# Gated cross-attention and a routed mixture of experts on one core: the two stages in one block, and the late logits read from where TensorE writes them

## The reference, cut to what matters

```python
x = x + jnp.tanh(g_xattn[0]) * xattn(ctx_1024, layernorm(x), ...)      # 8 x 112 x 256
t = layernorm(x)
logits = t @ Wg                                                        # 8 experts
P = softmax(logits); keep the two largest, P_norm = P_topk / (sum + 1e-9)
h = gelu(t @ W1[e] + b1[e]);  y_e = h @ W2[e] + b2[e]
x = x + jnp.tanh(g_ffn[0]) * sum_e P_norm[e] * y_e
```

## Time and profile before

| what | value |
|---|---|
| median of three runs | 502.27 us (501.06 to 504.05) |
| profiled execution, its own time | 500.76 us |
| its span (first to last instruction) | 499.0 us |
| mean granted TensorE clock | 0.931 of full speed |
| PE, DVE, ACT, POOL busy | 435.5, 286.8, 266.9, 198.3 us |

### The profile page before, as it was taken

One profiled execution on the slowest core, in us unless ns is written; L12 is line 12 of the kernel. 1 busy time (PEld: TensorE's weight loads), 2 busy tenths in 40 slices (PEclk: granted clock), 3 DMA queues, 4 the chain that ended last, 5 costly groups with the idle time before them and its releaser, 6 DMA issues. The chain is left out here.

```text
span 499.0 us, 9197 instructions
## 1 busy us (share of the span) xinstructions
PE 435.5 (87%) x3173; PEld 368.0 (74%) x3173; DVE 286.8 (57%) x707; ACT 266.9 (53%) x568; POOL 198.3 (40%) x219
## 2 busy tenths in 40 slices
PE   1899789999999999999995714899999999999990
PEld 1787557676767676767774513499999999999990
DVE  4654725363535444363447216298888888888840
ACT  3431147757575847566673110276776766676630
POOL 3440046555555565656402464002233333323222
PEclk9999979999999999999997555599999999999996
DMA  7300000001000199701700125586777878782313
GB/s 235 85 14 18 1 31 2 31 3 32 1 28 3 36 288 236 173 1 59 279 1 2 46 66 194 163 279 178 232 228 211 238 224 227 217 214 42 54 22 95
DMA packets 41864, 56.04 MB, mean 112 GB/s; under 512 B 1746, under 2 KB 37154, under 8 KB 41809
## 3 DMA queue, kind: packets, MB, share of 16 engines
q1 hardware_dynamic: 36848, 49.80, 32.6%
q0 software_dynamic: 4960, 5.72, 7.4%
q10 hardware_dynamic: 16, 0.00, 0.0%
HBM read 40.37 MB, written 16.07 MB: 113 GB/s over the span
## 5 line engine op out<-in xcount | busy, mean ns | idle before, releaser
L1379 POOL DMA_INDIRECT acc_scratch<-yv,xt x28 | 50.7, 1810 | 128.3 <-DVE yv L1532 124.0
L1401 ACT ACTIVATE hf<-ph,b1t 128x256 f32<-128x256 f32 x112 | 47.1, 472 | 47.9 <-PE ph L1607 47.2
L867 DVE TENSOR_REDUCE negmax<-sc 112x1 f32<-112x487 f32 x64 | 39.6, 660 | 49.5 <-PE sc L1115 49.5
L669 ACT COPY probt<-pt 125x448 f32<-125x448 f32 x64 | 34.3, 538 | 46.5 <-PE pt L1123 46.4
L661 ACT ACTIVATE prob<-sc,negmax 112x487 f32<-112x487 f32 x64 | 42.2, 664 | 24.9 <-DVE negmax L867 24.8
L1140 PEld LDWEIGHTS po<-probt,vals 125*64 125x64 f32 (+1 forms) x512 | 26.1, 142 | 23.0 <-issue 15.6
L1514 DVE TENSOR_TENSOR hl<-hf,hh 128x512 fp32r<-128x512 f32 x56 | 38.8, 692 | 1.9
L1123 PE MATMUL pt<-ident,prob 112*125 112x112 f32 x256 | 38.9, 276 | 0.0
L1123 PEld LDWEIGHTS pt<-ident,prob 112*125 112x125 f32 x256 | 36.0, 193 | 2.8
L1512 DVE CAST hh<-hf 128x512 fp32r<-128x512 f32 x56 | 24.2, 432 | 23.4 <-ACT hf L1401 23.0
L374 POOL TENSOR_TENSOR krot<-krow,rope_t 125x512 f32<-125x512 f32 x21 | 26.7, 1273 | 24.4 <-ACT krow L617 24.4
(11 more groups left out here) (303 smaller groups left out, 1295.2 us busy)
## 6 DMA issues: line engine op xcount, KB each, us to landing
w_first<-in_L_ffn_W SPq DMA_DIRECT2D x10, 1024.0 KB, 8.0
w_next<-in_L_ffn_W SPq DMA_DIRECT2D x10, 1024.0 KB
rows_scratch<-blank SPq DMA_DIRECT2D x2, 4257.0 KB, 32.2
w_third<-in_L_ffn_W SPq DMA_DIRECT2D x8, 1024.0 KB, 7.9
xt<-rows_scratch SPq DMA_DIRECT2D x14, 258.0 KB, 2.8
ctx_t<-in_ctx SPq DMA_DIRECT2D x8, 375.0 KB
w_first<-in_L_xattn_Wkv SPq DMA_DIRECT2D x1, 1024.0 KB, 9.2
x_all<-in_x SPq DMA_DIRECT2D x2, 448.0 KB, 4.1
```

The source lines that it names most:

```text
L669: act.copy(probt[:, h // 2 % 2, :, h % 2, :], pt[h % 2][0:JR, 0:NT * M].rearrange("q (a r) -> q a r", a=NT)) \
L867: dve.tensor_reduce(negmax[:, h % 2:h % 2 + 1], sc[h % 2][0:M, 0:JA], AX, ALU.max, negate=True).then_inc(max_done.sem, 1)
L1379: pool.indirect_dma_start(out=acc_dram, out_offset=bass.IndirectOffsetOnAxis(ap=xt[i % 3][:, n, D + 1:D + 2].bitcast(I32), axis=0), in_=yv ...
L1401: last = act.activation(hf[:, n % 3, u], ph[n % 3][:, u * T:(u + 1) * T], ACT.Gelu, bias=b1t[:, col])
```

## The change

Both functions now return their five instruction streams instead of opening a block; `build_program` opens one block, in which each engine runs its stream of attention and then its stream of experts. All semaphores are allocated in the outer scope. The memory that experts lays over attention's is guarded by two waits, whose values `attention` returns in `over_at`: SP waits for the last projection through Wo before it loads `b1rows`, and POOL waits for the last logits before it clears `b2x`. DVE no longer copies the late logits to `logit`; it runs `pick_first` on them in `pv`, at the end of attention's stream.

```diff
-        logit = keep("logit", [M, 2, E])
...
+        of_attention, over_at = attention(nc, sem, x, ctx, g_xattn, ...)
+        of_experts = experts(nc, sem, over_at, w1, b1, w2, b2, ...)
+        block = whole.enter_context(nc.Block())
+
+        @block.sync
+        def _(sp):
+            of_attention[0](sp)
+            of_experts[0](sp)
...
-        block = st.enter_context(nc.Block())
...
                 dve.wait_ge(logit_done, B)
-                dve.tensor_copy(logit[:], pv[0:M, (B - 2) * E:B * E].rearrange("q (b e) -> q b e", e=E))
+                router.pick_first(dve, pv[0:M, (B - 2) * E:B * E].rearrange("q (b e) -> q b e", e=E), LATE, 1)
...
+        last = B // 2 - 1, 1
+        over_at = dict(projected=(wo_done.sem, wo_done.at(*last, 1)), logits=(logit_done, B))
+        return (sync, gpsimd, scalar, vector, tensor), over_at
...
-        block = st.enter_context(nc.Block())
-        @block.sync
-        def _(sp):
+        def sync(sp):
+            sp.wait_ge(*over_at["projected"])
             sp.dma_start(b1rows[:], b1.rearrange("e (f p) -> (e f) p", p=P)).then_inc(small_loaded, 16)
...
             pool.memset(upto[:], 1.0).then_inc(ptables_set, 1)
+            pool.wait_ge(*over_at["logits"])
             pool.memset(b2x[:], 0.0).then_inc(b2x_set, 1)
...
-            router.pick_first(dve, logit[:], LATE, 1)
             router.pick_second(dve, LATE, 1)
```

More of the change, by code:

```diff
@@ L192, in build_program, with _, attention @@
         weights |= {n: [sem(f"{n}{r}") for r in range(RING)] for n in ("w1_loaded", "w2_loaded")}
-        attention(nc, x, ctx, g_xattn, g_ffn, gamma_x, beta_x, gamma_l, beta_l, wq, wkv, wo, rope,
-                  wg, w1, w2, x_all, x2, tokh, tokl, ident, gates, neg_half, ws, wn, w1s, w2s, w1n, w2n, wide, deep, logit,
+        of_attention, over_at = attention(nc, sem, x, ctx, g_xattn, g_ffn, gamma_x, beta_x, gamma_l, beta_l, wq, wkv, wo, rope,
+                  wg, w1, w2, x_all, x2, tokh, tokl, ident, gates, neg_half, ws, wn, w1s, w2s, w1n, w2n, wide, deep,
                   rows_dram, blank, rows1, rows2, router, **weights)
[L196 to L201, removed]
+        of_experts = experts(nc, sem, over_at, w1, b1, w2, b2, out, rows_dram, acc_dram, x_all, rows1, rows2, router, ident, gates, w1s, w2s, w1n, w2n, wide, deep,
+                **weights)
+        block = whole.enter_context(nc.Block())
[3 more added lines that the diff above has]
+            of_experts[0](sp)
+        @block.gpsimd
+        def _(pool):
+            of_attention[1](pool)
+            of_experts[1](pool)
+        @block.scalar
+        def _(act):
+            of_attention[2](act)
+            of_experts[2](act)
+        @block.vector
+        def _(dve):
+            of_attention[3](dve)
+            of_experts[3](dve)
+        @block.tensor
+        def _(pe):
+            of_attention[4](pe)
+            of_experts[4](pe)
+def attention(nc, sem, x, ctx, g_xattn, g_ffn, gamma_x, beta_x, gamma_l, beta_l, wq, wkv, wo, rope,
+              wg, w1, w2, x_all, x2, tokh, tokl, ident, gates, neg_half, ws, wn, w1s, w2s, w1n, w2n, wide, deep,
               rows_dram, blank, rows1, rows2, router, w1_loaded, w2_loaded, w1h_done, w1l_done, w2h_done, w2l_done, filled):
@@ L210, in ps @@
             return st.enter_context(nc.psum_tensor(name, [P, 512], F32))
-        def sem(name):
-            return st.enter_context(nc.semaphore(name))
         def tally(name, per):
@@ L419, in _, with gpsimd @@
                 sp.dma_start(to2[:], w2[e].rearrange("(f p) d -> p f d", p=P)).then_inc(w2_loaded[e], 16)
-        @block.gpsimd
-        def _(pool):
+        def gpsimd(pool):
             for c in (crstd_done, cl_done, rope_done, krow_done, orstd_done, row_copied, x1_kept):
@@ L553, in _, with scalar @@
             frame(pool, prepare, latents, lambda t, p: None, head, close)
-        @block.scalar
-        def _(act):
+        def scalar(act):
             for c in (cf_done, ch_done, kraw_done, keys_done, vals_done, exp_done, probt_done, out_done):
@@ L731, in _, with vector @@
             frame(act, prepare, latents, begin, head, close)
-        @block.vector
-        def _(dve):
+        def vector(dve):
             for c in (cstat_done, cparts_done, cvar_done, cnorm_done,
@@ L955, in close, with tensor @@
                 dve.wait_ge(logit_done, B)
-                dve.tensor_copy(logit[:], pv[0:M, (B - 2) * E:B * E].rearrange("q (b e) -> q b e", e=E))
+                router.pick_first(dve, pv[0:M, (B - 2) * E:B * E].rearrange("q (b e) -> q b e", e=E), LATE, 1)
             frame(dve, prepare, latents, begin, head, close)
-        @block.tensor
-        def _(pe):
+        def tensor(pe):
             for c in (ctr_done, kproj_done, vproj_done, ktr_done, score_done,
@@ L1240, in _, with experts @@
             frame(pe, prepare, latents, begin, head, close)
-def experts(nc, w1, b1, w2, b2, out, rows_dram, acc_dram, x_all, rows1, rows2, router, ident, gates, w1s, w2s, w1n, w2n, wide, deep,
-            logit, w1_loaded, w2_loaded, w1h_done, w1l_done, w2h_done, w2l_done, filled):
+        last = B // 2 - 1, 1
+        over_at = dict(projected=(wo_done.sem, wo_done.at(*last, 1)), logits=(logit_done, B))
+        return (sync, gpsimd, scalar, vector, tensor), over_at
+def experts(nc, sem, over_at, w1, b1, w2, b2, out, rows_dram, acc_dram, x_all, rows1, rows2, router, ident, gates, w1s, w2s, w1n, w2n, wide, deep,
+            w1_loaded, w2_loaded, w1h_done, w1l_done, w2h_done, w2l_done, filled):
     with ExitStack() as st:
@@ L1644, in _ @@
             down(TILES - 1, 3)
+        return sync, gpsimd, scalar, vector, tensor
 def rope_table(np):
```

## The result

| | before | after |
|---|---|---|
| median of seven runs | 501.60 us (501.06 to 504.05) | 498.45 us (497.56 to 499.41) |
| profiled execution | 500.76 us | 497.56 us |
| span | 499.0 us | 495.8 us |

The ratio of after to before is 0.9929 (95% interval 0.9908 to 0.9950): 3.15 us less by the medians, 3.2 by the profiled executions. The forecast was 4.9 less. The direction and the range held; over a third of the gain that was forecast did not come. The forecast of 497.4 stood on the median of three runs, 502.27; the seven runs put the kernel before at 501.60. Measured 498.45 lies midway between the forecast and rival 1's 499.5.

What follows compares the result with a forecast made beforehand. The seam between the stages was taken to decide the gain, the tiles being TensorE-bound and untouched. 4.95 at `place` less 0.1 for the collision gave 4.85, rounded to 4.9: 502.27 - 4.9 = 497.4 us, range 494.9 to 500.2.

Steps and rivals of the forecast that it cites:

- rival 1: Row tile 1 to 3 us late from harder scatter-weight collision or a slower DVE step; gain about 2.8, time 499.5; chance 0.12.
- four links at the seam: Between the stages: barrier, `b1rows` load, PE's late-slot sums, then the chain through DVE to b2 matmuls and first tile.
- `b1rows` hidden under attention: Load issued after the last Wo projection, landing at about 288.4, covered until 295.16: costs nothing, with 6.8 to spare.
- `place` 4.95 earlier: DVE's `place` step starts at 300.0 instead of 304.95, with DVE, no longer PE, the later one: gain 4.95.
- the two guards costing nothing: SP's wait for the last Wo projection and POOL's wait for the last logits would each cost 0.
- the PSUM reads costing nothing that shows: Three steps of `pick_first` reading the late logits in `pv` would cost between 0 and 0.06, taken as 0.03.
- the collision: Before the first row tile, late scatters share DMA engines with 2 MB of `w_third` weights: delay 0 to 1.1, taken as 0.1.
- rival 3: First row tile load queues among 2 MB of weights, landing in 10.5 against 3.6; 6.9 lost, time 504.3; chance 0.05.
- the 14 tiles as long as before: Sign expected in the changed profile: the expert tiles, bounded by TensorE and untouched by the change, keep their duration.
- A later rise: TensorE's clock rises 3 us later in the first tile, costing 1.3: 498.7; chance 0.06.
- the 2.77 and the 2.19: At the seam, without the barrier, DVE starts 2.77 earlier and POOL's small memsets 2.19 earlier.
- Rival 4: The 2.2 at the seam goes to fetching the next stage's instructions, not the barrier, and stays: about 502.3; chance 0.04.

Runs made afterwards that it cites:

- barrier_b1_early: The kernel before, barrier and logit copy kept, with only `b1rows` loaded at the end of attention into a dead buffer; median 500.19 us, ratio 0.9964.
- logit_copied: The changed kernel, but the late logits are first copied to SBUF and the router reads the copy; median 498.32 us, ratio 0.9936.
- rstd_between: The changed kernel, with POOL scattering items 0 to 2 before the last variance step and 3 to 5 after it; median 496.90 us, ratio 0.9896.
- The two moved loads: Two kernels, each the changed kernel with `w_third`'s weight loads moved: behind the first two row tiles (497.71 us, 0.9917), or to about 286 us (497.14 us, 0.9905).
- third_early_warm: The changed kernel with `w_third` loaded at about 286 us, plus 20 useless matmuls where PE waits for pT; median 497.11 us, ratio 0.9908.
- third_early: The changed kernel, with the two weight loads of `w_third` issued directly behind `b1rows`, at about 286 us; median 497.14 us, ratio 0.9905.
- two_barriers: The kernel before, with a second block of one tiny memset between the stages, so the engines meet twice; median 501.96 us, ratio 1.0005.
- quiet_barrier: The kernel before, barrier kept, with POOL's two scatters of item 5 issued behind the barrier instead of in front; median 499.16 us, ratio 0.9953.
- rstd_and_third: The changed kernel with scatters of items 3 to 5 behind the last variance step and `w_third` loaded at 286 us; median 494.92 us, ratio 0.9870.
- all_three: rstd_and_third plus 24 useless matmuls where PE waits for pT; median 492.61 us, ratio 0.9839 against the kernel before.

## Why the prediction was right, and where it was too large

**Right, step by step.** The path (four links at the seam, tiles untouched), `b1rows` hidden under attention, PE's sums 5.5 earlier, DVE as the next one late, `place` 4.95 earlier (5.03), the two guards costing nothing, the PSUM reads costing nothing that shows. `barrier_b1_early` and `logit_copied` bear out the two terms that can be taken apart: 2.3 at `place` for the load, 0.2 for the copy.

**Mis-sized: the collision.** In the sum this is the term of 0.1 that is taken from 4.95. The step put the delay of the scatters at 0.1 and its upper bound at 1.1. It measured 1.6, and 0.8 of it reached PE. I had seen the place, and the margin shrink from 3.3 to 0.5, but bounded the delay by an estimated landing of the weights at 308.8. The error was to let the weights land at their old pace while they share the engines with more scatters (after, the engines are busy with them to about 309.6), and to argue from POOL's pace of issue, which says nothing about landing. From 309.6 to the tile load at 311.23 it is 1.6, as if the last scatter had begun only then, which is the mechanism of the upper bound. It is no rule: in `rstd_between` the tile load left 0.2 to 0.3 behind the weights. The two moved loads show it, and `rstd_between`, with 5.3 from the last scatter to the tile load, shows how far the collision can go. The Trainium skill, page DMA: Bandwidth & Descriptors, section Queues, rings and completion order, has the engines take packets of the queues in turn. That was set against a delay; 1.6 us, and 3.6 in `rstd_between`, say that turns with a queue of 2 MB of weights are not cheap for a scatter. Rival 1 named this mechanism with 1 to 3 us; it came true at 0.8. A second misreading softened it. The 3.6 of the tile load was taken for its landing, so both paths seemed to end within 0.1 of each other with no slack; the load had landed in 2.8, and the slack of about 0.8 took up half of the delay. That the gain did not fall below rival 1's 2.8 is owed to a slack that I had not counted, and is luck. The figure of 3.6 stands in rival 3 too, where 2.8 belongs.

**Mis-sized: the clock, and "the 14 tiles as long as before".** A later rise was a rival at 0.06. Over all profiles the rise stood 3.3 to 6 behind the first `up`, and each us of it cost 0.45 in the tiles, near the 0.4 of the prediction. In the profiled pair 0.35 of the 0.6 is this. The other 0.25 goes with the missing barrier and is not explained. The longest tiles beyond that, `logit_copied` and `third_early_warm`, have PE idle for 0.6 and 0.3 in them. The profile before, at 3.5, was near the earliest rise that any kernel showed, so the sum made against it likely came out high by some tenths. In `third_early`, at 5.7, only 0.4 of the 1.0 gained at the first `up` arrived at the last matmul. The Trainium skill, page TensorE: Matmul & The Clock Gate, section Part 1, calls the moment of the rise "run-variable". The one program profiled twice here rose at 4.3 and 4.1, so these runs do not show it; whether the moment depends on the program's own timing stays open.

**Wrong in the picture, not in the sum: the barrier.** Both the 2.77 and the 2.19 were right as distances. That they are the price of a barrier was not: `two_barriers` puts the meeting at 0.3, and `quiet_barrier` the rest on POOL's side: its scatters in flight, or a fixed time behind its last instruction. Rival 4 rightly said that the 2.2 might be spent by something other than the barrier, but named another thing, and took for granted that it would stay. It went with the barrier.

## What to carry to other kernels

Before taking a barrier away, look at what POOL does last in front of it: the barrier ended 2.1 to 2.3 us behind POOL's last instruction, and cost 0.3 where POOL had been idle that long. Moving two scatters and a copy out of its way brought most of what taking it away did. When an edit moves two DMAs by different amounts (2.2 and 5.0 here), ask what they now meet, and price it by landing, not by issue; bulk loads belong where no small transfer is waited for. A gain just ahead of dense TensorE work is only as good as the clock's rise behind it, so compare several profiles before booking its last us.

## What the runs showed of the hardware that I had not expected

- Where POOL's memset of `b2x` (64x2048, 1.79 us) ran beside DVE's cast of 112x4 elements, the cast took 2.13 (`rstd_between`), 1.45 (`rstd_and_third`) and 1.43 (`all_three`) instead of 0.17, and ended within 0.05 of the memset. In the other direction, POOL's third late scatter took 2.07 instead of 0.95 in the kernel before and after, where it overlaps DVE's 128x1024 subtraction (1.21). These are overlaps in the traces; no run took the one away alone.
- The clock rose among 24 matmuls of 128 rows (4.5 us of them) in `all_three` and about 1 us behind 20 of them in `third_early_warm`, while eight b2 matmuls of 64 rows, 7.2 us without a pause, never raised it; once high, it stayed high through the same eight.
